# A fused adaptive-mixing and LoRA feed-forward kernel: x1 loaded from ScalarE's queue, and the gathers' row numbers computed later

## The reference, cut to what matters

```python
y      = einsum('bct,bcd->bdt', x, weights[condition])        # per batch 32x32 mixing
result = einsum('bnd,od->bno', y, W_base) + b_base
logits = einsum('bnd,ed->bne', y, W_gate)                      # 8 experts, top 2, softmax over them
h      = einsum('bnd,erd->bner', y, A)                         # 8 experts x rank 16
delta  = einsum('bner,eor->bno', h * route_w, B)
out    = x + result + delta * (16 / 16)
```

## Time and profile before

| | |
|---|---|
| median of 3 runs | 95.09 us (94.37, 95.09, 96.64) |
| the profiled execution | 94.81 us, span 93.0 us |
| TensorE, matmuls / weight loads | busy 89.2 us (96%) / 85.8 us (92%) |
| VectorE | 65.6 us (71%) |
| ScalarE | 23.2 us (25%) |
| GpSimd | 15.8 us (17%) |
| TensorE's granted clock | full in all 40 slices |
| DMA | 10.65 MB, mean 115 GB/s |

### The profile page before, as it was taken

One profiled execution on the slowest core, in us unless ns is written; L12 is line 12 of the kernel. 1 busy time (PEld: TensorE's weight loads), 2 busy tenths in 40 slices (PEclk: granted clock), 3 DMA queues, 4 the chain that ended last, 5 costly groups with the idle time before them and its releaser, 6 DMA issues.

```text
span 93.0 us, 1814 instructions
## 1 busy us (share of the span) xinstructions
PE 89.2 (96%) x642; PEld 85.8 (92%) x642; DVE 65.6 (71%) x229; ACT 23.2 (25%) x55; POOL 15.8 (17%) x29
## 2 busy tenths in 40 slices
PE   6998999999999999999999999999999999999980
PEld 1596999999999999999999999999999999999970
DVE  2887987767675767767675767867675968867660
ACT  2265621312213040312213040312213040311210
POOL 5178103300304040210304040210400000000000
PEclk9999999999999999999999999999999999999999
DMA  1999272422507070322507050332608020302023
GB/s 35 316 307 375 66 217 104 151 93 95 137 1 230 9 210 23 129 104 85 148 0 233 7 204 28 116 120 75 162 7 226 0 113 0 112 8 113 0 113 113
DMA packets 6369, 10.65 MB, mean 115 GB/s; under 512 B 1017, under 2 KB 1625, under 8 KB 6361
## 3 DMA queue, kind: packets, MB, share of 16 engines
q1 hardware_dynamic: 5480, 10.11, 33.2%
q0 software_dynamic: 448, 0.23, 1.2%
q10 hardware_dynamic: 432, 0.20, 0.8%
HBM read 6.35 MB, written 4.19 MB: 113 GB/s over the span
## 4 chain that ended last, share of the span: by engine, by line
PE 87%; DMA 6%; SPq 2%; DVE 1%; ACT 1%; issue 0%
PE main_ps L538 52%; PE y_ps L525 13%; PE main_ps L554 11%; DMA w_raw<-w_all 6%; PE main_ps L616 5%; PE main_ps L622 3%; PE hwT_ps L548 2%; SPq L218 1%; SPq L215 1%; DVE x_sb L506 1%; ACT w_hi L289 1%; PE main_ps L655 0%; SPq L220 0%
## 5 line engine op out<-in xcount | busy, mean ns | idle before, releaser
L538 PE MATMUL main_ps<-w_hi,y_hi 128*128 128x320 f32 x112 | 26.9, 322 | 0.3 <-ACT w_hi L289 0.3
L538 PE MATMUL main_ps<-w_lo,y_hi 128*128 128x320 f32 x112 | 26.7, 320 | 0.0
L538 PE MATMUL main_ps<-w_hi,y_lo 128*128 128x320 f32 x112 | 25.6, 310 | 0.0
L265 POOL DMA_INDIRECT mixw<-cond_w,row_ids x14 | 13.7, 975 | 48.2 <-PE y_ps L525 46.0
L538 PEld LDWEIGHTS main_ps<-w_hi,y_lo 128*128 128x128 f32 x112 | 19.0, 188 | 0.0
L538 PEld LDWEIGHTS main_ps<-w_hi,y_hi 128*128 128x128 f32 x112 | 17.9, 189 | 0.9 <-ACT w_hi L289 0.9
L538 PEld LDWEIGHTS main_ps<-w_lo,y_hi 128*128 128x128 f32 x112 | 18.4, 188 | 0.2
L525 PE MATMUL y_ps<-mix,x_sb 128*128 128x128 f32 x124 | 16.7, 277 | 0.0
L525 PEld LDWEIGHTS y_ps<-mix,x_sb 128*128 128x128 f32 x124 | 15.8, 193 | 0.1
L299 ACT ACTIVATE second<-top 128x1 f32<-128x1 f32 x16 | 4.7, 295 | 42.1 <-DVE top L404 42.1
L431 DVE TENSOR_TENSOR hwT_lo<-hwT_ps,hwT_hi 128x128 fp32r<-128x128 f32 x16 | 4.7, 292 | 13.3 <-ACT hwT_hi L306 13.3
(11 more groups left out here) (67 smaller groups left out, 86.8 us busy)
## 6 DMA issues: line engine op xcount, KB each, us to landing
x_sb<-x SPq DMA_DIRECT2D x16, 256.0 KB, 3.0
out<-x_sb SPq DMA_DIRECT2D x15, 256.0 KB, 2.0
w_raw<-w_all SPq DMA_DIRECT2D x4, 324.0 KB, 5.1
b_raw<-b_lora SPq DMA_DIRECT2D x1, 256.0 KB, 5.8
bias_sb<-bias SPq DMA_DIRECT2D x1, 256.0 KB, 3.7
mixw<-cond_w,row_ids POOLq DMA_INDIRECT x14, 2.5
out<-x_sb ACTq DMA_DIRECT2D x1, 128.0 KB, 1.8
out<-x_sb SPq DMA_DIRECT2D x1, 128.0 KB, 1.8
```

What stands on the lines that cost most here:

```text
L265: pool.indirect_dma_start(mixw[:, t, :], None, cond_w, bass.IndirectOffsetOnAxis(row_ids[:, t:t + 1], 0))\
L538: last = pe.matmul(main_ps[t % 2][:, half, 0:n_cols], y, w[:, half * HALF:half * HALF + n_cols], start=i == 0, stop=i == STEPS - 1)
```

## The change

x1 leaves SyncE's list and is issued by ScalarE between the table and `cond_sb`. `row_ids` moves on VectorE from between select(0) and select(1) to behind the two low halves of tile 0. Nothing else differs, and the same instructions are run.

```diff
@@ block.sync
             load_x(0)
             load_w(0)
-            load_x(1)
             load_w(1)
             load_w(2)
             load_w(3)
@@ block.scalar
             act.dma_start(table[:, 0, :, :], cond_w.rearrange("(p k) d -> p k d", k=K)).then_inc(table_landed, 16)
+            act.dma_start(x_sb[:, 1, :], x_tiles[1, :, :]).then_inc(x_landed[1], 16)
             act.dma_start(cond_sb[:, :], cond).then_inc(cond_landed, 16)
@@ block.vector
             select(0)
-            dve.wait_ge(cond_landed, 16)
-            dve.wait_ge(channel_ready, 1)
-            dve.scalar_tensor_tensor(out=row_ids[:, :], in0=cond_sb[:, :], scalar=float(C),
-                                     in1=channel[:, 0:1].to_broadcast([P, TILES]),
-                                     op0=ALU.mult, op1=ALU.add).then_inc(rows_ready, 1)
             select(1)
             low_w(0)
             for (y, hi, lo), have, ready in zip(first_halves(), (first_y_hi_ready, y_hi_ready),
                                                 (first_y_lo_ready, y_lo_ready)):
                 dve.wait_ge(have, 1)
                 dve.tensor_tensor(lo, y, hi.bitcast(f32), ALU.subtract).then_inc(ready, 1)
+            dve.wait_ge(cond_landed, 16)
+            dve.wait_ge(channel_ready, 1)
+            dve.scalar_tensor_tensor(out=row_ids[:, :], in0=cond_sb[:, :], scalar=float(C),
+                                     in1=channel[:, 0:1].to_broadcast([P, TILES]),
+                                     op0=ALU.mult, op1=ALU.add).then_inc(rows_ready, 1)
             high_w_rest()
             low_w(1)
```

## The result

The change made the kernel a little slower: 95.48 us median against 94.97 us, 22 runs each, ratio 1.0059 with a 95% interval of 1.0037 to 1.0082, so +0.35 to +0.78 us. That is within the 2% that were to be told from no change. The ratio leaves out each kernel's executions that are over 1.5% above its own quickest, which puts the limit at 95.8 us for the kernel before and at 96.3 us for the change; the plain means are 0.56 us apart as well, without the one execution of the change that took 310.4 us. No run shows why that one did, nor why one of the kernel before took 112.85 us in a later comparison, at a granted clock of 0.76.

A forecast was written before the change was run, and what follows sets the result against it. The prediction took tile 1's start on TensorE as the bound; VectorE's 0.0 and ident's +0.3 us on 94.81 gave 95.1, median put at 95.2, forecast 94.9 to 95.5, with 94.2 to 96.2 to hold 8 in 10.

The forecast's parts named there:

- What bounds the kernel: TensorE runs without a gap behind the first tile, so only tile 1's start (11.28) matters; ceiling of a gain 0.96 us.
- (1) w0 later by 0.62: DMA queues: x1 competes with x0 and w0, so w0 lands at 5.54 instead of 4.92, +0.62 us.
- the rival of a longer delay: DMA: the slow stretch falls ahead of w0's end, w0 at 6.0, total 95.6, up to 96.0; chance 0.2.
- (2) w1 sooner: SyncE's queue: w1 issued 0.46 us sooner, landing between 7.43 and 6.5; worth at most VectorE's idle 0.67 us.
- (3) The two cancel on VectorE: VectorE's chain: w0's delay and row_ids are paid out of idle time and w1's gain, 0.0 to +0.1 us.
- (4) ident: GpSimd: later row_ids makes ident ready at 11.27, TensorE waits ahead of tile 1; +0.15 to +0.55, taken as +0.3 us.
- (5) gather(2) lands in time: GpSimd's gather: landed at 10.8, before select(2) wants it at 11.29; cost 0.
- The sum: Whole kernel: 0.0 for VectorE plus 0.3 for ident, +0.3 us on 94.81, thus 95.1; median put at 95.2.
- The rival of a gather late by microseconds: DMA: gather(2) lands at 13.5, holding up select(2) and tile 2's mixing, about +2 us, 96.9; chance 0.04.
- That of a starving x1: DMA: x1 gets no share and lands at 9, all 3 us later, 98; chance 0.03.

The follow-up runs named there:

- e1: The change again without an edit, against the kernel before: ratio 1.0065, 12 runs; profiled execution 94.96 us.
- e12: The change once more without an edit, against the kernel before: ratio 1.0032, 12 runs, lowest 94.86 us.
- e2: The change with ident and expert_ids made on GpSimd before its wait for the row numbers; ratio 1.0010 to the kernel before.
- e5: The change with ident and expert_ids made behind gather(4) instead of ahead of it; ratio 1.0113 to the kernel before, 6 runs.
- e11: The same kernel as e2 once more, run beside e12 on one chip; ratio 1.0021 to the kernel before.
- e7: The kernel before with x1 on ScalarE's queue and ident made before the gathers, row_ids in its old place; ratio 0.9967, 6 runs.
- e8: The kernel before, unaltered, against itself: ratio 0.9969, 6 runs, lowest 94.72 us.
- e3: The kernel before with only row_ids moved behind the low halves of tile 0, x1 still on SyncE's queue; ratio 1.0041.
- e6: The kernel before with row_ids moved and ident made before the gathers, x1 on SyncE's queue; ratio 0.9980, 6 runs.

## Why the prediction was right, and where its size was off

*What bounds the kernel.* Right: only the start of tile 1 matters, and 81.7 to 81.9 us follow it in every profile.

*(1) w0 later by 0.62.* Right in size for ordinary executions: the high part of w0 starts at 5.38 to 5.85 in the eight profiles of the experiments with x1 on ScalarE's queue (5.51 in e1), predicted 5.54. In the profile that came with the result it starts at 6.33, past even the 6.0 of the rival of a longer delay; what made it so late there is open. x0 slipped further than the 4.74 that I allowed in two of the nine: in that profile, and in e12, where TensorE waited 0.42 us for it and began to mix at 5.13. In e12 the chain on VectorE hung on w0 and not on x0, so that cost nothing more.

*(2) w1 sooner.* Better than the far end of my bounds, 6.5: w1 was issued at 2.03 and landed 4.4 later, at 6.43 (e1); in e12 it took 4.8. (Its issue came 0.48 sooner by the prediction's own two times, not 0.46.) ScalarE takes it up at 6.68, as soon as it is through with y.

*(3) The two cancel on VectorE.* Right against the profile of before, and the slack was used as described: no idle time in 7.04 to 10.50. Predicted were 7.95 for the end of `row_ids`, 8.31 for L386 and 10.8 for the last low part; e1 has 7.87, 8.10 and 10.50, e12 has 8.20, 8.44 and 10.84, before had 10.78. Against the quickest executions of the kernel before it doesn't cancel, as the sum below shows.

*(4) ident.* The mechanism is right and its time within 0.03: `ident` ready at 11.24, predicted 11.27, and e2, e5 and e11 turned the wait off and up. The gathers took 1.12 and 1.00 beside the low parts, not 1.18 each. The first step of tile 1 I had at 11.5; it came at 11.29, because the steps ahead of it were 0.17 quicker. By TensorE's own pace the term is what I took it for, +0.3: 0.18 of waiting and 0.11 for the restart.

On the rule of the Trainium skill (SBUF — State Buffer, the "DVE blocks DMA" trap) the trace of the change decides nothing: L386 ends at 8.10 and gather(2) begins at 8.15, 0.28 behind `row_ids` as in the kernel before, and takes the same 1.12 as the first gather there, so the two didn't overlap and the 0.40 that the rule could have added was not at stake. In e7 they do overlap: L386 lies inside the second gather, and neither is longer than elsewhere.

```profile
7.52 0.94 POOL L264 DMA_INDIRECT mixw<-cond_w,row_ids  x1 [0.30 <-issue]
...
7.67 0.32 DVE L386 CAST w_hi<-w_raw 128x328 fp32r<-128x328 f32 x1
```

*(5) gather(2) lands in time.* Right: the bias, issued on its landing, goes out at 10.72, so it landed by then, predicted 10.8. The rival of a gather late by microseconds falls with it. That of a starving x1 falls by its own rows: x1 landed 3.5 us after its issue in e1 and 4.3 in the slowest profile.

*The sum.* Predicted +0.3 for this term and for the whole, measured +0.56 (+0.35 to +0.78). Over the three comparisons of the change together its mean is 0.37 us higher (95.49 us from 45 executions, against 95.12 from 102 of the kernel before, the two outliers left out), nearer to the prediction. The median of 95.48 is in the range, but my 95.2 didn't follow from my own working: the three runs shown had a median of 95.09, and with 0.3 that is 95.4.

The sum has a step that is too simple, and a single profile hides it. I priced the wait against the profiled execution, whose tile 1 started at 11.28. The quickest executions of the kernel before take 94.2 us; less the 1.8 us by which the device time exceeds the span (94.81 - 93.0) and the 81.8 us behind the start of tile 1, tile 1 starts at about 10.6 in them, an estimate. For these a floor at 11.24 costs 0.6 us, and the change's lowest times (94.86 to 94.92) against 94.21 to 94.37 show it. Not all of that is `ident`: with the wait gone (e2, e11) the lowest time is 94.59, so `ident` is 0.3 of it, and the rest fits the chain on VectorE, which in the change begins later with w0 and holds `row_ids`. That second floor is read from rows and from lowest times; no run turns it off and on.

On the mean both floors are cheap. Raising the 102 ordinary times of the kernel before to at least 94.6 gives +0.04 us, to at least 94.9 +0.14 us. In addition the floor of `ident` moves: `row_ids` stands behind w0 and the mixing, and where these are late (e12, and at 12.73 in the profile that came with the result) `ident` is late with them, 0.1 to 0.2 us behind TensorE's own pace each time. That makes 0.2 to 0.3 us together; what is left is 0.2 to 0.3 of the 0.56, or at most 0.1 of the 0.37. It is of the size of what e2 and e11 still show over 1, and of their noise, and it stays open. So the mechanism was forecast and shown; that its size came out so near is in part luck, as the spread of the executions was not in the sum.

## What to carry to other kernels

When an instruction is moved to a later place, follow not only its consumer but everything that stands behind that consumer in program order on the consumer's engine: here a 0.17 us instruction on VectorE held back two gathers, and behind them an identity matrix that needs none of them. Setup that depends on nothing goes ahead of the first wait. A slack of 3 us that is spent to the last tenth becomes a floor, which costs most in the executions that would have been quick and nothing in those that are long anyway; price it against the spread of the times, not against one profile.

## What the runs showed that I had not expected

The mixing matmuls of tile 0 took 275 ns each in one execution and 421 ns in another of the same kernel, though the row of the granted clock reads 1.00 (the full level, 2.4 GHz) in both. From the profile of before and from that of e8, matmuls of the second half of tile 0: count, least, median and most in ns.

```profile
L525 PE MATMUL hwT_ps<-mix,x_sb x4: 275/275/275, 5.5 to 5.9; 128*128 128x128 f32 x4
```

```profile
L525 PE MATMUL hwT_ps<-mix,x_sb x4: 421/421/421, 5.8 to 6.5; 128*128 128x128 f32 x4
```

Ahead of them TensorE did the same work in both. It put the first main step at 6.78 and 7.67, and still tile 1 started at 11.28 and 11.33: in the one TensorE waits for weights on the way, in the other it doesn't. Where the mixing is slower still, in the 96.01 us of e2, that cover is used up and the end moves; what sets the pace of the mixing is open. And the slow microsecond of the DMA engines at 4.90 to 5.90 (212, 276, 315 and 372 GB/s in before, e3, e8 and e6) belongs to no instruction that was moved here.
